# Graph attention with a layer norm: the positive sums of a step ahead of its negative ones, and TensorE's passes written out

## What is computed

```python
xt  = jnp.einsum('ni,hio->hno', x, W)            # x: 8192 x 256, 4 heads of 64
src = jnp.einsum('hnf,hf->hn', xt, a[:, :out_f])
dst = jnp.einsum('hnf,hf->hn', xt, a[:, out_f:])
e   = jax.nn.leaky_relu(src[:, :, None] + dst[:, None, :], NEG_SLOPE)
e   = jnp.where((adj_matrix > 0)[None, :, :], e, -jnp.inf)
h_prime = jnp.einsum('hij,hjf->hif', jax.nn.softmax(e, axis=2), xt)
...
out = _layernorm(x + h_prime.transpose(1, 0, 2).reshape(n, heads * out_f))
```

## Time and profile before

| | us |
|---|---|
| median of 3 runs | 2275.49 |
| lowest and highest run | 2274.74, 2275.79 |
| the profiled execution | 2278.14 |
| its span, first to last instruction | 2275.9 |
| PE busy in the span | 2080.7 (91%) |
| DVE busy | 2098.8 (92%) |
| ACT busy | 2011.4 (88%) |
| POOL busy | 126.9 (6%) |

### The profile page before, as it was taken

One profiled execution on the slowest core, in us unless ns is written; L12 is line 12 of the kernel. 1 busy time (PEld: TensorE's weight loads), 2 busy tenths in 40 slices (PEclk: granted clock), 3 DMA queues, 4 the chain that ended last, 5 costly groups with the idle time before them and its releaser, 6 DMA issues.

```text
span 2275.9 us, 79541 instructions
## 1 busy us (share of the span) xinstructions
PE 2080.7 (91%) x34180; PEld 2051.7 (90%) x34180; DVE 2098.8 (92%) x2334; ACT 2011.4 (88%) x2045; POOL 126.9 (6%) x88
## 2 busy tenths in 40 slices
PE   7702799999999999999999999999999999999996
PEld 6601799999999999999999999999999999999996
DVE  4587999999999999999999999999999999988785
ACT  2235699899999999999999999999999999999995
POOL 0063000001000000001000100001000100000000
PEclk9955999999999999999999999999999999999998
DMA  8746967776776667666766667666766667523310
GB/s 293 244 165 254 350 207 242 249 236 198 233 239 208 210 213 246 220 212 206 242 221 211 202 212 244 220 215 208 245 213 214 209 210 252 182 77 83 100 50 20
DMA packets 236578, 469.69 MB, mean 206 GB/s; under 512 B 14656, under 2 KB 23104, under 8 KB 236224
## 3 DMA queue, kind: packets, MB, share of 16 engines
q1 hardware_dynamic: 231600, 447.53, 60.2%
q0 software_dynamic: 4352, 16.78, 2.0%
q10 hardware_dynamic: 272, 0.13, 0.0%
HBM read 438.83 MB, written 25.56 MB: 204 GB/s over the span
## 4 chain that ended last, share of the span: by engine, by line
PE 49%; DVE 16%; ACT 15%; issue 8%; DVEq 1%; POOL 0%; ACTq 0%; POOLq 0%
PE acc L760 46%; ACT big L394 14%; DVE big L566 5%; DVE big L573 5%; PE tp L725 2%; DVE nat L488 1%; ACT big L412 1%; DVE big L558 1%; DVE stats L619 1%; DVE AT L502 1%; DVE big L580 1%; DVE nat L486 1%; ACT big L406 0%; DVE big L588 0%; DVE big L605 0%
## 5 line engine op out<-in xcount | busy, mean ns | idle before, releaser
L394 ACT ACTIVATE big<-big,d_all 128x1024 int8<-128x1024 f32 x1792 | 1896.0, 1141 | 92.0 <-PE acc L760 89.4
L760 PE MATMUL acc<-big 128*128 128x130 f16 x32768 | 1917.5, 220 | 26.4 <-DVE big L580 18.1
L760 PEld LDWEIGHTS acc<-big 128*128 128x128 fp8e5 x32768 | 1892.6, 98 | 37.5 <-issue 33.4
L566 DVE SCALAR_TENSOR_TENSOR big<-big,AT 128x1024 uint32<-128x1024 uint32 x512 | 624.1, 1219 | 74.1 <-ACT big L394 66.3
L573 DVE SCALAR_TENSOR_TENSOR big<-AT,big 128x1024 uint32<-128x1024 uint32 x512 | 623.4, 1218 | 4.5
L725 PE MATMUL tp<-ident,nat 128*128 128x128 f32 x1024 | 157.1, 276 | 130.4 <-DVE nat L486 112.8
L725 PEld LDWEIGHTS tp<-ident,nat 128*128 128x128 f32 x1024 | 109.8, 142 | 136.4 <-issue 130.1
L558 DVE TENSOR_SCALAR big<-big,d_all 128x1024 uint8<-128x1024 f32 x256 | 191.8, 749 | 0.0
L486 DVE TENSOR_SCALAR nat<-raw 128x2048 fp8e4<-128x2048 int32 x128 | 176.3, 1380 | 10.2 <-DMA raw<-in_adj_dram 9.8
L488 DVE TENSOR_SCALAR nat<-raw 128x2048 uint8<-128x2048 int32 x128 | 177.4, 1386 | 0.0
L502 DVE SCALAR_TENSOR_TENSOR AT<-AT,tp 128x512 uint32<-128x512 uint32 x224 | 153.3, 684 | 1.5
(11 more groups left out here) (48 smaller groups left out, 370.3 us busy)
## 6 DMA issues: line engine op xcount, KB each, us to landing
raw<-in_adj_dram SPq DMA_DIRECT2D x256, 1024.0 KB, 5.5
big<-v_parts SPq DMA_DIRECT2D x512, 260.0 KB, 3.7
v_parts<-big SPq DMA_DIRECT2D x16, 1040.0 KB, 4.2
big<-s_rows SPq DMA_DIRECT2D x32, 512.0 KB, 5.5
AT<-in_x_dram SPq DMA_DIRECT2D x16, 512.0 KB, 4.1
big<-in_x_dram POOLq DMA_DIRECT2D x8, 1024.0 KB, 7.9
out_dram<-big POOLq DMA_DIRECT2D x8, 1024.0 KB, 8.5
big<-in_L_gnn_W_dram SPq DMA_DIRECT2D x2, 128.0 KB, 2.5
```

The costliest lines, as they stand in the source:

```text
L394: return nc.scalar.activation(sgn[:, g % NB, b, :], srow[:, h % 2, :], ACT.Sign, bias=dflat[:, r:r + 1], scale=-1.0)
L566: nc.vector.scalar_tensor_tensor(out=word(sgn, g % NB), in0=word(sgn, g % NB), scalar=EDGE[plane], in1=edges(g), op0=ALU.bitwise_and, op1= ...
L760: return nc.tensor.matmul(acc[:, k, o:o + 2 * VO], m[:, g % NB, b, t * P:(t + 1) * P], Vr[:, v:v + 2 * VO], start=opens, stop=False, skip_ ...
```

## The change

`sums` now waits first for `pos_done`, the first mask of the step, and for `v_in`. In the middle steps 1 to 14 the loop over `cd` goes outermost: the 32 matmuls of the positive half come first, then stands a wait for `neg_done` (with a small semaphore instruction of its own), then come the 32 of the negative half. Steps 0 and 15 wait for both masks ahead of their matmuls and keep their order. `sums_done` is still counted by the last matmul of the step. The two hardware loops around PE's passes 4 to 27 and 28 to 31 become Python loops, so all 32 passes stand in PE's list one after the other, with waits on constants. The lines behind line 17 move up by one. No other engine's list changes.

```diff
--- before.py
+++ after.py
@@ -15,7 +15,6 @@
     ALU = mybir.AluOpType
     ACT = mybir.ActivationFunctionType
     AX = mybir.AxisListType
-    PE = [mybir.EngineType.PE]
     RMAX = bass.bass_isa.ReduceOp.max
 
     P = 128
@@ -746,7 +745,7 @@
             pe.wait_ge(sT_done, 1)
 
             def sums(p, g):
-                pe.wait_ge(neg_done, p * NG + g + 5)
+                pe.wait_ge(pos_done, p * NG + g + 1)
                 pe.wait_ge(v_in[g], 16 * p + 16)
                 pe.sem_inc(pe_passed, 1)
                 opened = set()
@@ -761,6 +760,8 @@
                                             start=opens, stop=False, skip_group_check=True)
 
                 if g in (0, NG - 1):
+                    pe.wait_ge(neg_done, p * NG + g + 5)
+                    pe.sem_inc(pe_passed, 1)
 
                     for t in range(T):
                         if g == 0 and t in (0, 3, 6):
@@ -772,8 +773,11 @@
                         if g == NG - 1 and t in (2, 5):
                             ins.then_inc(part_done, 1)
                 else:
-                    for b in range(B):
-                        for cd in range(2):
+                    for cd in range(2):
+                        if cd:
+                            pe.wait_ge(neg_done, p * NG + g + 5)
+                            pe.sem_inc(pe_passed, 1)
+                        for b in range(B):
                             for t in range(T):
                                 ins = add(b, cd, t)
                 ins.then_inc(sums_done, 1)
@@ -786,9 +790,9 @@
 
             for h in range(H):
                 one_pass(h, lambda g, h=h: [(UN + k, k % UN) for k in made_at(True, h * NG + g)])
-            with nc.Fori(H, NP - H, engines=PE, hint_back_edge=True) as p:
+            for p in range(H, NP - H):
                 one_pass(p, lambda g: [((p + H) * HALF + g // 2, g // 2)] if g % 2 == 0 else [])
-            with nc.Fori(NP - H, NP, engines=PE, hint_back_edge=True) as p:
+            for p in range(NP - H, NP):
                 one_pass(p, lambda g: [])
```

## The result

| | before | changed |
|---|---|---|
| median of 20 runs each | 2275.78 | 2271.65 |
| lowest, highest | 2272.82, 2280.68 | 2268.91, 2273.0 |
| the profiled execution | 2278.14 | 2272.27 |
| its span | 2275.9 | 2270.7 |
| PE busy | 2080.7 | 2074.1 |

The ratio of the times is 0.9979, with a 95% interval of 0.9972 to 0.9986: 4.8 us less, between 3.2 and 6.4. The lines of the changed kernel are one lower, so L759 is the sums, L724 the transposes, L572 the second mask, L579 DVE's part sums, L393 and L405 ACT's signs and part sums.

A forecast was written before the change was run, and what follows sets the result against it. Busy shares named no bound; PE held 49% of the chain, and DVE without idle time set the next pass's start. Terms 0 + 0 + 0 + 3.2 us took 2275.49 to 2272.3 us, range 2267.0 to 2277.0, chance 0.64.

The forecast's parts named there:

- The positive sums first: Step 10 of every fourth pass: sums start 0.75 us earlier, but PE waits as much longer at next g = 0; zero.
- Rival (a): Waits for the second mask are on the path: 9.2 us gain in all, 2266.3 us; chance 0.14.
- The price of the new order: Middle steps: 448 added semaphore instructions and inner waits cost zero, at most 0.045 us per wait; no gain named.
- Rival (c): Inner wait in 448 middle steps is not hidden, costing PE 0.045 us each: 2283.6 us; chance 0.09.
- The back edges: PE's two loops: removing 26 taken back edges gains zero, since most leave no mark or only lengthen a later wait.
- rival (d): Each of PE's 26 taken back edges hides a 2.84 us stop: 74 us less, 2202 us; chance 0.02.
- The stop near 2013: Between PE's two loops, 2.84 us of "issue" and a low clock go; through ACT's waits the gain is 3.2 us.
- The point where the last four passes begin: Sign near 2010: the prediction is wrong if this point moves by more than 1 us.
- all before them as long as now: Sign: passes before the last four keep their length, while the last four get about 3 us shorter.

The follow-up runs named there:

- e1_order: Kernel before with the new order of sums and the second wait in mid-step, both hardware loops kept; 2387.88 us, ratio 1.0484.
- x2_pad: Kernel before with 20 more semaphore increments in each loop round, old order and loops kept; 2373.65 us, ratio 1.0436.
- x1_before: The kernel before, unchanged, profiled again; 2276.3 us in one run.
- x4_shift: Kernel before with 20 semaphore increments once ahead of the first loop, rounds as long as before; 2278.49 us, ratio 1.0014.
- e4_tail_out: Kernel before with only its second loop (passes 28 to 31) written out; 2273.6 us, ratio 0.9995.
- e5_first_out: Kernel before with only its first loop (passes 4 to 27) written out; 2275.42 us, ratio 1.0004.
- e2_unroll: Kernel before with both PE loops written out, old order and single wait kept; 2273.25 us, ratio 0.9991.
- x3_order_loops: Kernel before with only the loop over the halves outermost in middle steps, loops and one wait kept; 2272.3 us, ratio 0.9985.
- e3_onewait: Changed kernel, but waiting for both masks ahead of every step, without the second wait; 2271.79 us, ratio 0.9985 to before.
- e0_changed: The changed kernel itself, measured and profiled once more beside the first group of experiments; 2271.04 us, ratio 0.9984 to before.
- e8_dve_out: Changed kernel with DVE's one loop of two rounds written out as well; 2268.97 us, ratio 0.9974 to before.
- e7_nohint2: Kernel before with both loops, but no back-edge hint on the second one; 2284.56 us, ratio 1.0042.

## Why the prediction came out as it did

All kernels of the old round length side by side (the stretches as above; e1_order and x2_pad left out):

| kernel | order of sums | both loops kept | to pass 3 | passes 4 to 27 | the rest |
|---|---|---|---|---|---|
| before | old | yes | 497.7 | 1513.1 | 265.1 |
| x1_before | old | yes | 496.2 | 1513.0 | 265.4 |
| x4_shift | old | yes | 494.7 | 1515.1 | 265.8 |
| e4_tail_out | old | no | 495.0 | 1513.6 | 261.7 |
| e5_first_out | old | no | 495.0 | 1514.2 | 262.4 |
| e2_unroll | old | no | 496.3 | 1513.9 | 261.7 |
| x3_order_loops | new | yes | 497.3 | 1511.3 | 263.7 |
| e3_onewait | new | no | 495.7 | 1512.6 | 261.7 |
| changed | new | no | 496.2 | 1512.9 | 261.6 |
| e0_changed | new | no | 496.3 | 1511.3 | 261.9 |
| e8_dve_out | new | no | 495.4 | 1510.4 | 261.5 |

The stretch of 24 passes carries single stops of its execution. Whole chunks without one tell the halves of the change apart more finely. From the last matmul of pass 7 to that of pass 11 and from pass 19 to pass 23, in us:

| kernel | order of sums | wait ahead of the positive sums | passes 8 to 11 | passes 20 to 23 |
|---|---|---|---|---|
| before | old | both masks | 251.65 | 251.70 |
| e2_unroll | old | both masks | 251.69 | 251.69 |
| x3_order_loops | new | both masks | 251.39 | 251.38 |
| e3_onewait | new | both masks | 251.39 | 251.39 |
| e0_changed | new | first mask | 251.39 | 251.41 |

The new order is worth 0.3 us in a chunk, with loops and without. The wait for the first mask alone and the written-out passes are worth 0.04 at most.

**The positive sums first: zero. Right, and for the reason given.** The 0.54 us before step 10's sums went and came back at the next g = 0, which waits 0.66 us more. Rival (a) would have shown no longer wait there. The prediction misread one thing: of its eight waits for the second mask six stand at step 10, of passes 4, 8 and so on to 24, and two in pass 2. That changes nothing in a sum of zeros. e3_onewait, the same kernel without the early start, is slower by 0.75 us of medians, inside both intervals, where (a) wanted 6.0, and its chunks are as long to 0.02 us, where (a) wanted some 0.75.

**The price of the new order: zero. This is the step that failed.** The prediction split it into the inner wait and the loop order and wrote "Below zero there is no row to name a gain by". The inner wait is indeed free: e0_changed, which has it, and e3_onewait, which has not, spend the same time on a chunk. But the order brought a gain. The rows say how large: from 641.93 to 680.52 five middle pairs with their transposes took 38.59 us in the kernel before (the pairs of the earlier trace rows), from 640.34 to 678.84 they take 38.50. That is 0.09 / 10 = 9 ns for a step of 64 matmuls; between two matmuls of a middle step the mean distance went from 56.83 to 56.69 ns. Over 448 middle steps it is 4.0 us of PE's time, and by the share of 0.56 that the prediction used for the part on the path 2.3 us. x3_order_loops changes nothing else and shows 1.8 us in the middle stretch and 3.4 (1.4 to 5.7) by the ratio; 0.3 us in each of 8 chunks are 2.4. The reasoning that failed was this: a middle pair has no idle time, therefore nothing can be gained in it. A matmul's own pace was taken as fixed. Rival (c) was in the right place with the wrong sign.

**The back edges: zero. Right for the kernel before, but not the whole of what they are for.** e2_unroll's middle stretch is no shorter than before's. At the start of pass 6, where the kernel before had 0.72 us of "issue" at the edge, the changed one waits 0.85 us for L579 instead, as forecast. The prediction looked at the edges of the old loop only. With the change's own additional instructions the same loop cost 110 us (e1_order), so writing the passes out is what makes the split wait affordable. The Trainium skill's page "Runtime: NRT & Kernel Launch", section "Instruction fetch mechanics", on which rival (d) stood, says that a taken branch out of the current window stalls for a fetch. The trace of before did not agree; e7_nohint2 (3.2 us for each edge) and e1_order and x2_pad (a stop of 1.8 to 5.5 us at each of 23 edges) do. What the page says fits here for an edge without a hint and for the lengthened round; the hinted edges of the kernel before, with 0 to 1 us, are an exception that it does not name.

**The stop near 2013: gone, 3.2 us. Right.** No stop, no clock of 0.50 behind it, ACT's two waits for PE (3.0 and 0.2 us) gone, the rest of the span shorter by 3.5 us (3.2 in e0_changed). A low clock does come later, unforecast: after PE's wait of 3.17 us at the start of pass 30 the granted clock is 0.50 from 2130.7 to 2133.7. e8_dve_out has the same wait without the low clock, and its rest of 261.5 puts the price at 0.4 us or less. All kernels without the pair of loops have 261.5 to 262.4 there. It was read as code that had not arrived. What the profiles show is that among kernels with the old length of a round it stands where one hardware loop leads directly into another and not where either is written out; that it is a fetch stays an inference.

**The point where the last four passes begin** moved by 1.8 us, from 2010.8 to 2009.1, more than the 1 us by which the prediction called itself wrong. 1.5 of these were there by pass 3, as they were in the second profile of the kernel before; what is left, 0.3, is the gain of 1.8 less a stop that cost about 1.5 and that e0_changed does not have. So "all before them as long as now" was wrong by that gain. The test was badly set: an absolute time carries the scatter of the start, the length of a stretch does not.

**The value.** 3.2 us were forecast and 4.8 (3.2 to 6.4) measured. The missed gain of about 2 us makes the sum 5.5; the forecast's 3.2 lies at the interval's edge, with one term missing, and the interval would bear both sums. That the term was this small was luck: no step of the prediction had bounded it.

**Open, in full or in part.**

- Why the matmuls' pace depends on the order. The records say where it does. A step is eight groups of eight matmuls, each group with its own columns of the table. Averaged over 336 middle steps of the kernel before, the first matmul of a group takes 60.8 ns in six of the seven changes of group and 56.6 at the change to the third block; x3_order_loops has 59.1 to 60.0 in four of seven changes (to the second and the fourth block, in either half) and 56.7 in the others. The change from the positive half to the negative one is among those with 56.7, so it is not the changes between the halves as such. The two orders also walk their weights in another sequence, and no run separates weights from table.
- Why e5_first_out and, less so, e2_unroll and e4_tail_out gain less by the ratios (-0.9, 2.0 and 1.1 us) than at the end of their profiles, which all show about 3 us there; e5's interval leaves 3.2 out. Part of it is in e5's own profile, whose passes 4 to 27 are 1.1 us longer than before. A profile shows one execution, and single executions do differ in their stops, as at 885.
- The 0.8 us that e2_unroll's middle is longer lie in two chunks, 0.4 in each; the four others are as long as before to 0.04 us. It is not a price of every written-out pass.

## What to carry to other kernels

An engine without idle time, here DVE, swallows what its neighbours gain; look for it before counting removed waits. "No idle time" on the engine that bounds is not "nothing to gain": compare the length of like groups in two orders, since the pace of back-to-back matmuls can move by fractions of a nanosecond that add up. After adding instructions to a hardware loop, read the time at its back edges again. On PE keep the hint, and write the loop out when its edges begin to stop the engine; a loop of few rounds on DVE can be worth writing out too.

## What the runs showed of the hardware that was not expected

- A PE loop of 2169 recorded instructions a round passes its hinted back edges with 0 to 1 us of idle time; with 20 more it stops 1.8 to 5.5 us at each of 23, 99 to 110 us in all. Twenty instructions ahead of the loop instead cost 3 us.
- The hint of a back edge was worth 3.2 us for each one taken (e7_nohint2, three edges of the second loop).
- Two hardware loops one directly after the other stopped PE for about 3 us between them in four profiles out of four with the old length of a round; with either written out there was no such stop, and with longer rounds (e1_order, x2_pad) none either.
- One taken back edge of DVE's loop cost DVE 2.9 us and the kernel 2.1 to 2.4.
- The same 64 matmuls of a step take 9 ns less when both halves of the table are worked through one after the other instead of by turns, and only the order differs; the difference sits in the first matmuls of some groups.
